# A fused DiT block with cross-attention: new issue orders for all five engines, the first MLP product one stage per PSUM bank, the second in four pieces

## The reference

```python
m = silu(cond) @ w_ada + b_ada                      # nine vectors per element: shifts, scales, gates
h = ln(x) * (1 + sc_msa) + sh_msa                   # "w": attention in two windows of 128 tokens, 16 heads
x = x + g_msa * (softmax(q k^T / 4) v @ w_so + b_so)
h = ln(x) * (1 + sc_mca) + sh_mca                   # "t": attention to ctx, 16 heads,
s = q k^T / 4; keep the 16 largest of 256 scores of each row; softmax over those
x = x + g_mca * (attn v @ w_co + b_co)
u = (ln(x) * (1 + sc_mlp) + sh_mlp) @ w_m1 + b_m1   # "m": 256 -> 2 x 1024
x = x + g_mlp * (silu(u[:1024]) * u[1024:] @ w_m2 + b_m2)
x = x + softmax(q k^T / 4) v @ Wp + bp              # "l": attention to ctx, 16 heads, with its own modulation
```

## Time and profile before

| | us |
|---|---|
| median of three runs (lowest, highest) | 1410.12 (1408.02, 1412.46) |
| the profiled execution's own time | 1412.02 |
| its span, first to last instruction | 1409.4 |
| busy PE, DVE, ACT, POOL | 1206.5, 1155.1, 994.4, 878.4 |

### The profile page before, as it was taken

How to read it: one execution, slowest core, us unless ns; L and a number is a source line. 1 busy time by engine, 2 the same in 40 slices (tenths; PEclk the granted TensorE clock), 3 DMA queues, 4 the chain that set the end, 5 groups by cost and what they waited for, 6 DMA issues and landing times. The chain is left out here.

```text
span 1409.4 us, 37816 instructions
## 1 busy us (share of the span) xinstructions
PE 1206.5 (86%) x13192; PEld 838.9 (60%) x13192; DVE 1155.1 (82%) x3823; ACT 994.4 (71%) x2001; POOL 878.4 (62%) x1161
## 2 busy tenths in 40 slices
...
DMA packets 111385, 67.17 MB, mean 48 GB/s; under 512 B 13836, under 2 KB 107870, under 8 KB 111198
## 3 DMA queue, kind: packets, MB, share of 16 engines
...
## 5 line engine op out<-in xcount | busy, mean ns | idle before, releaser
L1210 ACT ACTIVATE prob<-turned_score 128x1024 f32<-128x1024 f32 x320 | 326.5, 1020 | 113.3 <-PE turned_score L920 109.3
L1437 POOL TENSOR_TENSOR pair<-full,pair 128x512 f16<-128x512 f32 x192 | 221.7, 1159 | 154.8 <-ACT pair L1184 151.0
L1443 POOL TENSOR_SCALAR far<-far 128x512 bf16<-128x512 bf16 x256 | 158.0, 617 | 131.1 <-DVE far L1372 114.4
L1355 DVE MAX8 top<-score 128x8 f32<-128x256 f32 x512 | 193.5, 420 | 26.6 <-PE score L920 26.1
L1358 DVE MATCH_REPLACE8 rest<-top,score 128x256 f32<-128x256 f32 x512 | 208.3, 415 | 0.0
L1372 DVE MATCH_REPLACE8 far<-best,rest 128x256 bf16<-128x256 f32 x512 | 205.7, 410 | 0.2 <-issue 0.2
L1345 DVE TENSOR_REDUCE rowmax_l<-score 128x4 f32<-128x1024 f32 x128 | 156.2, 1220 | 54.2 <-PE score L920 40.8
L920 PE MATMUL work<-pair_n,w_m_hi 128*128 128x256 f16 x1024 | 172.7, 274 | 0.9 <-ACT other L1240 0.7
L920 PE MATMUL work<-pair_n,w_m_lo 128*128 128x256 f16 x512 | 140.1, 274 | 0.0
L1184 ACT ACTIVATE pair<-full 128x512 f16<-128x512 f32 x192 | 121.0, 630 | 23.6 <-DMA q_stack_l<-pair 6.6
L1422 POOL TENSOR_SCALAR rstd_n<-mean_var_n 128x2 f32<-128x2 f32 x64 | 12.8, 200 | 175.2 <-DVE mean_var_n L1337 172.6
...
## 6 DMA issues: line engine op xcount, KB each, us to landing
...
```

The costliest lines, as they stand in the source:

```text
L1210: act.activation(prob[:, at:at + 2, :], both_b[:, :, :], ACT.Exp).then_inc(exp_done, 1)
L1355: first = [step(dve.max(eight[:, t, :], bank[:, t * L:(t + 1) * L])) for t in range(LT)]
L1437: pool.tensor_tensor(pr[:, 1, :, :], whole[:, :, :], pr[:, 0, :, :], ALU.subtract).then_inc(split_lo, 1)
L1443: pool.tensor_scalar(tile, tile, FAR, -1.0, ALU.add, ALU.mult).then_inc(far_fixed, 1)
```

## The change

The tables, the element offsets and the shifts are all replaced, so that all five lists change. `m1` becomes eight pieces per element (one stage of 12 matmuls in one bank each; a bank is free again when the `mt` of its pair is done), and `m2` four pieces of 12 matmuls (index 0 and 1: the two halves of the output over the first half of the hidden values, 2 and 3 over the second), which share one bank taken at index 0. Pieces 0 and 1 wait for the first two `mh` and `ml` alone. A semaphore of its own, `m2_done`, tells `fo_m` and the next element's first `mh` that the product is done.

```diff
@@ the tables, the middle group's TensorE row as a sample @@
-    ("pe", "ot_t:0@17.84927 bk_t:0@20.92022 pr_t:0@27.32679 xt_t:0@30.87073 x4_n3:0@38.99526 m1:0@44.71247 "
-            "m1:1@48.13301 m1:2@56.66323 m1:3@65.57644 m2_0:0@77.64378 xt_m:0@80.89578"),
+    ("pe", "ot_t:0@20.10638 bk_t:0@23.4048 pr_t:0@27.90583 xt_t:0@30.66669 x4_n3:0@38.08485 m1:0@46.81186 "
+            "m1:1@47.07749 m1:2@49.83866 m1:3@50.2822 m1:4@60.39381 m1:5@61.5976 m1:6@68.97044 m1:7@68.99099 "
+            "m2:0@76.59059 m2:1@78.76153 m2:2@78.85847 m2:3@80.75055 xt_m:0@83.69323"),
...
-                   ("x4", "pj", "vj", "gd", "ot", "bk", "pr", "xt", "m1", "m2", "wp")]
-        d_keys = [k for k in d_users for _ in range(2 if k[0][:2] in ("ot", "m1") else 1)]
+                   ("x4", "pj", "vj", "gd", "ot", "bk", "pr", "xt", "m1", "wp") or k[0] == "m2" and k[2] == 0]
+        d_keys = [k for k in d_users for _ in range(2 if k[0][:2] == "ot" else 1)]
...
-                return tanh_done, HC // 2 * b + i + 1
+                return tanh_done, HC // 2 * b + i // 2 + 1
...
-                    for j in range(2):
-                        bank, n = d_take(piece, b, i, back=1 - j), 2 * i + j
-                        three_terms(bank[:, 0:L], W["m1"], slice(n * P, (n + 1) * P), own_pair["n3"], CC)
-                        m = three_terms(bank[:, L:2 * L], W["m1"], slice(HID + n * P, HID + (n + 1) * P),
-                                        own_pair["n3"], CC)
+                    bank = d_take(piece, b, i)
+                    three_terms(bank[:, 0:L], W["m1"], slice(i * P, (i + 1) * P), own_pair["n3"], CC)
+                    three_terms(bank[:, L:2 * L], W["m1"], slice(HID + i * P, HID + (i + 1) * P), own_pair["n3"],
+                                CC).then_inc(d_ready, 1)
+                elif kind == "m2":
+                    if b == 0 and i == 0:
+                        pe.wait_ge(lo_done, weight_count("m2"))
+                    c, half = i % 2, i // 2
+                    pe.wait_ge(hid_hi, HC // 2 * b + 2 * half + 2)
+                    pe.wait_ge(hid_lo, HC // 2 * b + 2 * half + 2)
+                    bank = d_take(piece, b, i) if i == 0 else d_bank("m2", b, 0)
+                    for k in range(HC // 2 * half, HC // 2 * (half + 1)):
+                        for n, (a, part) in enumerate((("hi", 0), ("hi", 1), ("lo", 0))):
+                            m = mm(bank[:, c * L:(c + 1) * L], W["m2"][a][:, k, c * P:(c + 1) * P], hid[:, part, k, :],
+                                   i == 0 and k == 0 and n == 0, i == 3 and k == HC - 1 and n == 2)
+                    if i == 0:
                         m.then_inc(d_ready, 1)
-                elif kind == "m2":
-                    if b == 0:
-                        pe.wait_ge(lo_done, weight_count("m2"))
-                    pe.wait_ge(hid_hi, HC // 2 * (b + 1))
-                    pe.wait_ge(hid_lo, HC // 2 * (b + 1))
-                    bank = d_take(piece, b, i)
-                    for c in range(CC):
-                        m = three_terms(bank[:, c * L:(c + 1) * L], W["m2"], slice(c * P, (c + 1) * P), hid, HC)
-                    m.then_inc(d_ready, 1)
+                    if i == 3:
+                        m.then_inc(m2_done, 1)
...
-                    src = "m2_0" if s == "m" else "pr_" + s
-                    act.wait_ge(d_ready, d_no[src, b, 0])
+                    src = "m2" if s == "m" else "pr_" + s
+                    if s == "m":
+                        act.wait_ge(m2_done, b + 1)
+                    else:
+                        act.wait_ge(d_ready, d_no[src, b, 0])
...
-                        act.wait_ge(d_ready, d_no["m1", b, i] - 1 + j)
-                        bank, n, slot = d_bank("m1", b, i, back=1 - j), 2 * i + j, 2 * (n2 % 2) + j
+                        act.wait_ge(d_ready, d_no["m1", b, 2 * i + j])
+                        bank, n, slot = d_bank("m1", b, 2 * i + j), 2 * i + j, 2 * (n2 % 2) + j
...
-                        act.wait_ge(d_ready, d_no["m2_0", b - 1, 0])
+                        act.wait_ge(m2_done, b)
```

More of the change, by code:

```diff
@@ new lines @@
+    ("pe", "x4_n1:0@-6.90706 pj_wq:0@-2.39993 pj_wk:0@4.1906 vj_w:0@6.71658 a_w:0@26.64525 a_w:1@29.95151 "
+            "gd_w:0@32.06858 a_w:2@32.07884 gd_w:1@32.31761 gd_w:2@34.56035 a_w:3@38.24856 b_w:0@38.32788 "
+            "o_w:0@40.56372 gd_w:3@41.01137 b_w:1@43.06835 b_w:2@45.03826 o_w:1@46.42386 o_w:2@48.26397 "
+            "b_w:3@49.43673 o_w:3@51.60005 ot_w:0@54.39099 bk_w:0@56.76485 pr_w:0@60.86232 xt_w:0@64.09604"),
+    ("act", "sp_n1:0@-5.60821 sp_wq:0@0.69514 sp_wk:0@4.47055 v_w:0@8.07868 gc_w:0@31.57295 gc_w:1@35.50605 "
+            "gc_w:2@38.34758 e_w:0@41.65703 gc_w:3@43.05115 os_w:0@43.2033 e_w:1@43.93529 e_w:2@46.48944 "
+            "os_w:1@48.5639 os_w:2@52.23033 e_w:3@52.69148 os_w:3@54.20941 sp_ws:0@58.10794 fo_w:0@63.30753"),
@@ L59 @@
+    ("dve", "bn_n1:0@-17.84269 rm_w:0@24.47919 rm_w:1@26.55546 rm_w:2@29.71092 rm_w:3@39.32701 nv_w:0@54.92831 "
+            "xa_w:0@62.38605"),
+    ("pool", "rs_n1:0@-19.44322 lo_n1:0@-8.8718 lo_wq:0@3.49632 lo_wk:0@11.63506 lo_ws:0@54.42283"),
 )
 TOP = (
[L62 to L68 removed]
```

805 lines of the change are left out of this document (402 added, 403 removed).

## The result

| | before | after |
|---|---|---|
| median of four runs (lowest, highest) | 1409.54 (1408.02, 1412.46) | 1353.42 (1348.54, 1358.33) |
| the profiled execution's own time, its span | 1412.02, 1409.4 | 1348.54, 1346.7 |
| start: up to `xa_w` of element 3 | 262.1 | 257.9 |
| twelve turns: `xa_w` of element 3 to that of element 15 | 916.1 | 874.7 |
| one turn, mean of six (`xa_w` of 5 to 11) | 76.10 | 72.18 |

The ratio is 0.960 (95% interval 0.9561 to 0.9638): 56 us less, where I had forecast 23 and a range that ended at 1369. The direction was right and the size was not. Against the profile of before the turns give 41.4 us, the end 17.2 and the start 4.2.

What follows compares the result with a forecast made beforehand. VectorE's list with its hand-overs was taken to set the turn; turns -27, start +4 and end 0 gave -23 against the profiled 1412.0, so 1389, and a median of 1387 us, range 1369 to 1411.

Steps and rivals of the forecast that it cites:

- What bounds the kernel: Steady turn: VectorE's list with the hand-overs sets the 76.15 us; the order of pieces can shorten it to 70.75 at most.
- Hand-overs: VectorE's waits for scores: 3.53 us a turn becomes 0.55 + 0.93 = 1.48, so -2.05; bounds 0 and -3.53.
- xa_w: VectorE's 0.76 us wait ahead of `xa_w`: covered by `t1:8` going first, half taken, -0.4 a turn; bounds 0 and -0.76.
- the floor of 70.75: VectorE's busy us in a turn, claimed to stay since no instruction on VectorE, ScalarE or POOL is added or taken away.
- m1 and m2 in pieces: TensorE's products cut into pieces of 1.34 us: cost and gain by itself nothing, paid where the hand-overs are.
- How many turns: Steady stretch of 12 turns, 11 counted as both ends are disturbed: 11 x 2.45 = -27 us.
- The end: Last two elements: more bare hand-overs but VectorE little busy, so 0; bounds -6 and +6.
- The start: Element 0's `bn_n1` behind chunk 13, `pj_wq` at 40.8, 6 us later, some returning: +4; bounds 0 and +10.
- Is there room on TensorE?: TensorE's busy time with waits on ScalarE makes 72.6 us a turn; the forecast turn of 73.7 stays 1.1 above.
- TensorE's waits on ScalarE: Rival, in the turns: more such waits each delay an `a`, losing 2 of the 2.45 us: 1409; chance 0.12.
- the POOL chain: Rival, in the turns: POOL's `mp:3` and `ml:2` ahead of `fx:14` hold `b_t:7`, slower: 1424; chance 0.10.
- the idle time goes nearly all: Rival, VectorE's turn: all but 2 us of the 5.21 idle go, -3.2 x 12 = -38, +2: 1374; chance 0.13.

Runs made afterwards that it cites:

- e10_xa_first: The kernel after, with `xa_w` ahead of `t1:8` again in eight elements, as before the change: 1358.45 us, a single run.
- e3_orders_only: The code of before with the new tables, `m1` in four whole pieces and `m2` in one: 1410.34 us.
- e5_m2_together: The kernel after, with the four pieces of `m2` side by side: 1387.86 us.
- e1_fillers: The kernel before, with `t2:10`, `t2:1` and `bn_n1` of VectorE put between readers that follow each other directly: 1432.59 us.
- e9_two_lists: The kernel before, with `t2:10` moved on VectorE and `gd_l:0`, `o_l:3` and `gd_t:2` moved on TensorE: 1414.4 us.
- e2_cut_only: The changed code with the tables of before, the pieces of `m1` and `m2` staying side by side: 1412.43 us.
- e13_together_end: The kernel after, with each two pieces of `m1` and the four of `m2` side by side in elements 12 to 15 alone: 1373.41 us.
- e8: The kernel after without the shifts of elements 12 to 15: 1376.54 us.
- e12: The kernel after, unchanged, timed again beside other versions: 1355.62 us.
- e7: The kernel before without the shifts of elements 12 to 15: 1437.61 us.

## Why the prediction was wrong

**What bounds the kernel: right.** VectorE's list with the hand-overs set the turn, and the turn fell with VectorE's idle time. The time went where I had said it would, and more of it did.

**"Hand-overs", -2.05 us a turn: right within 0.32, with wrong parts.** The score waits went from 3.53 to 1.80, so -1.73. I forecast 0.55 and 0.93 and found 0.87 and 0.56, and one more of 0.37 at `rm_w:2`, which has only `xa_l` (0.68) as cover. The order of sizes was turned round by one slip: I let `m1:5` and the hand-over add up, though `m1:5` (710.87 to 712.2) is done before `rm_l:2` ends at 712.26; and I overlooked `m1:4` ahead of `a_l:2`. The four turns that I priced at 0.55 take 0.63 in the steady stretch (`xt_w` at 717.79), which changed nothing.

**"xa_w" and what I left as it was: mis-sized, the first failed step.** I took -0.4 for `xa_w` and nothing for `xa_t` and `nv_t`. All three waits of the earlier trace rows went, 0.76 + 0.39 + 0.53 = 1.68 us. The last of them I had misnamed: at 784.08, behind `xa_t`, `t1:5` and `bn_n3`, it is `nv_w`, which waits for `ot_w`; `nv_t` comes at 770.01 without a wait. The reason that I gave for `xa_w`, `t1:8` ahead of it, doesn't carry it (`e10_xa_first`); ScalarE's `fo_w`, which I had named as a condition only, is earlier, by its new place ahead of `e_t:1`. "VectorE one `t2` more" I had written down and priced at nothing; which move took away the waits of `xa_t` and `nv_w` wasn't tested.

**"No instruction on VectorE ... is added or taken away, so the floor of 70.75 stays": wrong by 0.7.** VectorE's busy time fell to 70.08 in this turn (70.09 in the next) with the same instructions. With six pauses fewer that is 0.11 us a pause on average, on top of the idle time that the trace shows for it. The other versions go the same way, not to the hundredth: same turn, `e3_orders_only` has four waits and 69.96 busy, `e5_m2_together` four and 70.00, `e1_fillers` eight and 70.54, `e9_two_lists` eight and 70.65. The timeline fits this: `rm_l:1` starts at 704.58 and lasts 1.22, to 705.80, and the `t2` that follows it at once starts at 705.72, so 0.08 us before that; an instruction that has to wait has no such overlap. The 0.03 us beyond the 0.08 weren't traced. With the busy time as measured the sum closes: 1.73 + 1.68 + 0.67 = 4.08 of 76.15 - 72.08 = 4.07.

**"m1 and m2 in pieces: nothing by itself": right as worded, wrong as used, the second failed step.** By itself the cut is indeed worth nothing (`e2_cut_only`). But I went on that VectorE "has the cover in either list (`t2:0`, `t2:1`, `bn_n1`)" at `a_l:6`, and so took the whole gain of the hand-overs as due to the orders. The runs show otherwise: the new orders without the cut give 0.9 us of the 3.9. The cover at `a_l:6` in the old list was the price of the 5.34 us of `m2_0`; the new list spends those pieces at the bare hand-overs, and without the cut `rm_l:6` then waits 1.86 us (`e5_m2_together`). The sum of the turn wasn't hurt by this, its reasons were.

**"How many turns", 11: right.** The twelve turns gave 41.4 us, 10.6 times the 3.92 of a turn. Against the -27 of the forecast, the size of the turn makes 14 us of the miss.

**"The end", 0 with bounds of 6: the third failed step.** It gave -17.2 in the first profile and -11.6 in the second. I had looked at how busy VectorE is there (13.88 of 50 us) and concluded that hand-overs cost little. But VectorE's idle time there isn't free: it waits for pieces of TensorE, and with the pieces of `m1` and `m2` side by side in the last four elements the end is 11.9 us longer at the same granted clock, as much as the change brings (`e13_together_end`). The term that I set at nothing, "m1 and m2 in pieces", is what was missing here. The rest of the 17.2 goes with the clock, 0.92 in the first profile and 0.90 before.

**"The start", +4: mis-sized; it came out near nothing.** `pj_wq` came at 43.13, later than the 40.8 of the sum and the 39 to 42 that I gave; `xa_w` of element 0 came 6 us later than before (86.51 for 80.5), as forecast. But at element 3 nothing of it is left: -4.2 in one profile and +3.0 in the other, with the clock between them. The five profiles with the new start lists unchanged (after, `e8`, `e10`, `e12`, `e13`) have 260.9 us on average, the four with the old ones (before, `e1`, `e2`, `e7`) 260.5. So it is the bound "0, all of it returns" that held.

**"Is there room on TensorE?"** By plain occupancy with its waits the turn could fall to 72.6 us at most. It fell to 72.18, with TensorE busy 71.08 of 72.08 and its weight loads 49.66. The floor of 72.6 was none, since TensorE's waits on ScalarE (1.6 us) went too. The Trainium skill, Perfetto Trace Analysis, section Identifying the Most-Contended Engine, takes the weight loads' share and the share of the peak rate, not the matmuls' busy time, as the measure; by the weight loads (69%) there is room still, by plain occupancy 1.0 us. The turn fell by more than the 3.5 us that occupancy had allowed, but no version's mean turn went below 72.07, so whether TensorE holds it there stays open.

**The rivals.** Neither TensorE's waits on ScalarE nor the POOL chain came: in the turn TensorE waits 0.6 us for POOL's `normed` and for nothing else. The nearest was "the idle time goes nearly all" (2 us left of 5.21; 1.80 were), with its 1374 us. The range was too narrow below because its terms left out waits of the earlier trace rows and the busy time that goes with a wait, and because the end was held within 6 us.

| | forecast | first profile after | again |
|---|---|---|---|
| turns | -27 | -41.4 | -41.6 |
| start | +4 | -4.2 | +3.0 |
| end | 0 | -17.2 | -11.6 |
| sum, against the profile of before | -23 | -62.7 | -50.2 |

The two profiles lie at either side of the median's 56 us.
